# Decoder kernel, last stage: the first LayerNorm half before the feed-forward inside attention batch 3, the second layer's products between the first layer's tiles, and the last LayerNorm in parts of 512, 256 and 256 columns

## The reference

```
def _layernorm(x, axis=-1, eps=1e-05):
    m = mean(x); v = var(x)
    return (x - m) / sqrt(v + eps)

# last cross attention, per batch element (4 of them): query x, key and value ctx_512 (1601 rows, 64 wide)
q, k, v = query @ Wq + bq, key @ Wk + bk, value @ Wv + bv
out = softmax(q @ k.T) @ v
x = layernorm(x + out)

# last feed-forward: hidden width 512, no biases, a scale per output column
h = silu(tlin(x, w1)) * tlin(x, w2)
h = gelu(tlin(h, h1))          # exact gelu
h = gelu(tlin(h, h2))
x = layernorm(x + tlin(h, w3))
```

## Time and profile before

| what | value |
|---|---|
| median of three runs | 706.71 us |
| the profiled execution | 703.72 us |
| its span | 701.9 us |
| PE busy | 620.9 us (88%) |
| DVE, ACT, POOL busy | 527.3, 451.0, 205.6 us |
| batch 3 of the last attention | from about 609.5 to 623.6 us of the span |
| feed-forward and last LayerNorm | from about 623.6 us to the end |

### The profile page before, as it was taken

The page is one execution under the profiler, slowest core; times in us unless marked ns, Lnnn a source line. Parts: engine busy times, 40 slices in busy tenths (PEclk is TensorE's granted clock), DMA queues, the critical chain, the costliest instruction groups (busy, mean ns, idle before and its releaser), DMA issues. The chain is left out here.

```text
span 701.9 us, 13641 instructions
## 1 busy us (share of the span) xinstructions
PE 620.9 (88%) x5206; PEld 341.4 (49%) x5207; DVE 527.3 (75%) x706; ACT 451.0 (64%) x814; POOL 205.6 (29%) x277
## 2 busy tenths in 40 slices
PE   8989899999999999999999796998709999978996
PEld 5645433333334333333433375886205556646883
DVE  5369889999999999999945464999298557868432
ACT  3555578888898888888887432655771056566223
POOL 7224532344455577766740030000000000005000
PEclk9999989999999999999999978999968999999998
DMA  8258575555565554544210287451000010000000
GB/s 204 95 148 267 172 227 173 140 116 138 161 157 121 124 138 98 116 96 97 66 36 1 70 299 312 151 166 59 0 2 0 0 46 1 1 1 1 0 1 30
DMA packets 43293, 70.74 MB, mean 101 GB/s; under 512 B 12492, under 2 KB 31652, under 8 KB 42720
## 3 DMA queue, kind: packets, MB, share of 16 engines
q1 hardware_dynamic: 31696, 38.34, 21.0%
q0 software_dynamic: 10928, 29.32, 13.5%
q10 hardware_dynamic: 608, 2.25, 1.4%
HBM read 44.41 MB, written 24.79 MB: 99 GB/s over the span
## 5 line engine op out<-in xcount | busy, mean ns | idle before, releaser
L962 ACT ACTIVATE prob<-ps 128x512 f32<-128x512 f32 (+2 forms) x480 | 253.1, 582 | 45.9 <-PE ps L738 38.8
L1083 DVE TENSOR_REDUCE pm<-ps 128x2 f32<-128x1024 f32 x192 | 225.8, 1215 | 6.6 <-PE ps L700 4.8
L761 PE MATMUL ps<-prob,vst 128*9 128x256 f32 (+1 forms) x1664 | 129.8, 384 | 10.2 <-ACT o_all L950 10.2
L738 PE MATMUL ps<-qq,kc 50*128 50x256 bf16 (+1 forms) x832 | 134.3, 275 | 0.1
L700 PE MATMUL ps<-kc,qq 48*128 48x512 bf16 x384 | 116.4, 388 | 2.9 <-DVE pm L1083 2.6
L738 PEld LDWEIGHTS ps<-qq,kc 50*128 50x128 bf16 (+1 forms) x832 | 52.1, 96 | 94.0 <-ACT prob L962 69.3
L761 PEld LDWEIGHTS ps<-prob,vst 128*9 128x9 f32 (+1 forms) x1664 | 25.1, 88 | 51.7 <-ACT prob L962 39.1
L1635 POOL DMA_DIRECT2D w_w<-in_w x2 | 1.1, 534 | 148.1 <-PE ps L1672 148.1
L1090 DVE TENSOR_REDUCE nm<-ps 128x4 f32<-128x512 f32 (+1 forms) x32 | 30.6, 958 | 14.9 <-PE ps L688 14.9
L700 PEld LDWEIGHTS ps<-kc,qq 48*128 48x128 bf16 x384 | 32.9, 93 | 13.2 <-DVE pm L1083 9.4
L688 PE MATMUL ps<-masks_b 64*128 64x256 bf16 x256 | 37.6, 269 | 0.0
(11 more groups left out here) (362 smaller groups left out, 1292.3 us busy)
## 6 DMA issues: line engine op xcount, KB each, us to landing
kc<-kc_scr SPq DMA_DIRECT2D x32, 300.2 KB, 5.0
comb_bc<-comb_scr SPq DMA_DIRECT2D x7, 512.0 KB, 4.7
below<-rden_scr POOLq DMA_DIRECT2D x13, 256.0 KB, 6.0
ctx<-ctx_scr POOLq DMA_DIRECT2D x1, 3204.0 KB, 15.0
raw<-in_wexp POOLq DMA_DIRECT2D x8, 384.0 KB, 3.9
exp_scr<-raw_high POOLq DMA_DIRECT2D x8, 384.0 KB, 3.5
exp_scr<-raw_low POOLq DMA_DIRECT2D x8, 384.0 KB, 4.4
kc_scr<-hi SPq DMA_DIRECT2D x6, 400.2 KB, 4.8
```

What stands on the lines that cost most here:

```text
L738: last = pe.matmul(bank[0:p, j * TQ:(j + 1) * TQ], kc[s][rows, j, t * 128:t * 128 + p], qq[s][rows, 0, j, :], start=(j == 0), stop=True, s ...
L761: last = pe.matmul(o_ps[32 * hh:32 * hh + VW, kind * TQ + q0:(kind + 1) * TQ], value[:, hh * VW:(hh + 1) * VW], prob[0:k, (NST * n + t) % ...
L962: act.activation(prob[0:p, g % P_RING, 2 * e:2 * e + 2, q0:TQ], s2[0:p, k % S2_RING, 0:2 * w].rearrange("p (i q) -> p i q", i=2), ACT.Exp, ...
L1083: dve.tensor_reduce(pm[:, m % 2, c, :, jt], banks, AX.X, ALU.max).then_inc(s1_read, 1)
```

## The change

1. `pe_ln5(0)` and `pe_ln5_v(0)`, with the Square on ACT, go from batch 3 into batch 2 (steps 4 and 5); Ln and Exp stay in batch 3, after step 0, and DVE's part goes from step 3 to step 1. Two weight pieces move: piece 5 from batch 3 step 0 to batch 2 step 4 (ACT) and from step 1 to batch 2 step 5 (DVE), piece 6 from step 1 to step 2 and from 2 to 3.
2. DVE does `gated(0)` (gate and high part of tile 0) before batch 3's reciprocal instead of after the residual.
3. up(2) goes before `pe_ln5(1)`, up(3) before `pe_ln5_v(1)`; behind it come tiles 0 and 1 of the first layer, interleaved: 24 matmuls that wait for one `ha_done` after the other. Only then up(4) to up(7). DVE's `dve_ln5(1)` and `split_x(1)` go from before gate 2 to before gate 4. The PSUM banks are dealt anew, and first-layer tile 2 waits for `full_done` 7, which is gate 6.
4. The last layer's half 0 (12 matmuls) goes before second-layer tile 6, its residual behind DVE's tile 5, ln6's centring of it between tiles 6 and 7, its Square on ACT before the last Gelu, its averaging behind tile 7. Half 1 is done in two parts of 256 columns: 24 matmuls of 256 columns in place of 12 of 512, two residuals, and each LayerNorm instruction twice at 256 columns. ACT runs Ln and Exp of half 0 first, with a table load for each, and goes back to the Ln table for the second half: four table loads where there were two. The store is three DMAs instead of two.

The core of the diff (`ln_parts` only learns to take a list of column ranges and views, `spans`):

```diff
-        HIGH_AT = {(1, 0): (0,), (1, 2): (1,), (1, 4): (2,), (2, 0): (3,), (2, 2): (4,), (3, 0): (5,), (3, 1): (6,)}
-        LOW_AT = {(1, 1): (0,), (1, 3): (1,), (1, 5): (2,), (2, 1): (3,), (2, 3): (4,), (3, 1): (5,), (3, 2): (6,)}
+        HIGH_AT = {(1, 0): (0,), (1, 2): (1,), (1, 4): (2,), (2, 0): (3,), (2, 2): (4,), (2, 4): (5,), (3, 2): (6,)}
+        LOW_AT = {(1, 1): (0,), (1, 3): (1,), (1, 5): (2,), (2, 1): (3,), (2, 3): (4,), (2, 5): (5,), (3, 3): (6,)}
-        UP, H1, H2, Y = ((0, 2), (4, 5), (6, 7)), (1, 3), (6, 7), (0, 2)
+        UP = ((0, 2), (4, 5), (1, 3), (0, 2), (1, 3), (6, 7), (0, 2), (1, 3))
+        UP_FREED = (None, None, None, 1, 3, None, 4, 5)
+        H1, H2 = (4, 5, 0, 2), (6, 7)
+        ends = [slice(0, CH), slice(CH, CH + CH // 2), slice(CH + CH // 2, 2 * CH)]
...
-                        if b == NB - 1 and p == 0:
+                        if b == NB - 2 and p == 4:
                             pe.wait_ge(s1_red, 2 * NB)
                             pe_ln5(0)
-                        if b == NB - 1 and p == 2:
+                        if b == NB - 2 and p == PAIRS - 2:
                             pe_ln5_v(0)
...
-                for k in range(1, len(tiles)):
-                    up(k)
-                    if k == 1:
-                        pe_ln5(1)
-                    if k == 2:
-                        pe_ln5_v(1)
...
+                def first_hidden(k):
+                    pe.wait_ge(ha_done, NM * (tiles[k][0] + 1))
+                    if k < 4:
+                        pe.wait_ge(full_done, 7)
+                    else:
+                        pe.wait_ge(g1_done, k - 3)
+                    for i in range(NM):
+                        done = hidden_part("h1w", ha, H1[k % 4], k, i)
+                    done.then_inc(h1_ps, 1)
...
+                def last_layer(n):
+                    end = ends[n]
+                    c = end.start // CH
+                    at = slice(end.start - c * CH, end.stop - c * CH)
+                    for i in range(NM):
+                        pe.wait_ge(hc_done, NM * c + i + 1)
+                        done = passes(Y[n], (high_w["w3"][:, i, :], low_w["w3"][:, i, :]), 0,
+                                      [part[:, i, at] for part in hc[c]], i == 0, i == NM - 1)
+                    done.then_inc(y_ps, 1)
+
+                up(1)
+                up(2)
+                pe_ln5(1)
+                up(3)
+                pe_ln5_v(1)
+                pe.wait_ge(full_done, 2)
+                for i in range(NM):
+                    pe.wait_ge(ha_done, i + 1)
+                    for k in range(2):
+                        done = hidden_part("h1w", ha, H1[k], k, i)
+                        if i == NM - 1:
+                            done.then_inc(h1_ps, 1)
+                for k in range(NM, len(tiles)):
+                    up(k)
+                for k in range(2, len(tiles)):
+                    first_hidden(k)
                 pe.wait_ge(split, split_by["h2w"])
...
+                for k in range(6):
+                    second_hidden(k)
+                last_layer(0)
+                second_hidden(6)
                 pe_ln(0)
+                second_hidden(7)
+                pe_ln2(0)
+                last_layer(1)
+                last_layer(2)
                 pe_ln(1)
-                pe_ln2(0)
+                pe_ln(2)
                 pe_ln2(1)
+                pe_ln2(2)
...
                 act.preload_act_table_set("natural_log")
-                act_ln(0)
-                act_ln(1)
                 act_log(0)
-                act_log(1)
                 act.preload_act_table_set(EXP_LN)
                 act_exp(0)
+                act.preload_act_table_set("natural_log")
+                act_ln(1)
+                act_ln(2)
+                act_log(1)
+                act_log(2)
+                act.preload_act_table_set(EXP_LN)
                 act_exp(1)
+                act_exp(2)
...
                     dve.tensor_copy(osb[:, b % 2, :], o_ps[:, 0:TQ]).then_inc(o_sb, 1)
+                    if b == NB - 1:
+                        gated(0)
                     dve.wait_ge(fin_ps, b + 1)
```

More of the change, by code:

```diff
@@ L112, in ln_parts @@
                 stack, *[f"{tag}_{n}" for n in ("centred", "squared", "var", "lnv", "rstd", "x")])
+            columns = spans or [slice(c * CH, (c + 1) * CH) for c in range(NCH)]
+            if not spans:
+                psum_c, psum_v = ([p[:, c, :] for c in range(p.shape[1])] for p in (psum_c, psum_v))
             def pe(c):
                 nc.tensor.wait_ge(r_ready, c + 1)
-                nc.tensor.matmul(psum_c[:, c, :], mean_out, R[:, c * CH:(c + 1) * CH],
+                nc.tensor.matmul(psum_c[c], mean_out, R[:, columns[c]],
                                  start=True, stop=True).then_inc(centred, 1)
@@ L1625, in _ @@
             def _(sp):
-                for c in range(NCH):
+                for c, end in enumerate(ends):
                     sp.wait_ge(x_ready, c + 1)
-                    sp.dma_start(out[:, c * CH:(c + 1) * CH], X[:, c * CH:(c + 1) * CH]).then_inc(stored, 16)
-                sp.wait_ge(stored, 16 * NCH)
+                    sp.dma_start(out[:, end], X[:, end]).then_inc(stored, 16)
+                sp.wait_ge(stored, 16 * len(ends))
             @block.gpsimd
@@ L1847, in _, with hidden_part @@
-                hidden("h1w", ha, ha_done, H1, g1_done, h1_ps)
-                pe.wait_ge(split, split_by["h2w"])
-                hidden("h2w", hb, hb_done, H2, g2_done, h2_ps)
-                for c in range(NCH):
-                    pe.wait_ge(hc_done, NM * (c + 1))
-                    for i in range(NM):
-                        done = passes(ps[:, Y[c], :], (high_w["w3"][:, i, :], low_w["w3"][:, i, :]), 0,
-                                      [part[:, i, :] for part in hc[c]], i == 0, i == NM - 1)
-                    done.then_inc(y_ps, 1)
+                def hidden_part(name, src, bank, k, i):
+                    c, m = tiles[k]
+                    return passes(ps[:, bank, :], (high_w[name][:, i, :], low_w[name][:, i, :]), m,
+                                  [part[:, i, :] for part in src[c]], i == 0, i == NM - 1)
@@ L2171, in row, with gated @@
                     dve.tensor_copy(shift[:, b % 2, :], fin[:, 0:TQ]).then_inc(row_sb, 1)
+                def gated(k):
+                    c, m = tiles[k]
+                    dve.wait_ge(sg_done, k + 1)
+                    if k >= 4:
+                        dve.wait_ge(ha_done, k - 3)
+                    dve.scalar_tensor_tensor(out=whole[:, k % 4, :], in0=ps[:, UP[k][1], :],
+                                             scalar=col[f"s2_{m}"], in1=sg[:, k % 2, :], op0=ALU.mult,
+                                             op1=ALU.mult).then_inc(full_done, 1)
+                    dve.wait_ge(full_done, k + 1)
+                    dve.tensor_copy(ha[c][0][:, m, :], whole[:, k % 4, :]).then_inc(high_done, 1)
                 phases(0)
```

87 lines of the change are left out of this document (43 added, 44 removed).

## The result

The changed kernel took 697.66 us (median of 11 runs, 694.63 to 700.88) where the kernel before took 704.30 us (11 runs, 700.82 to 708.05): a ratio of 0.9904, 95% interval 0.9875 to 0.9933. So the two traces agree with the sum and the runs do not, and most of what follows is about that difference.

A forecast was written before the change was run, and what follows sets the result against it. PE bounds the dense stretch (busy 55.50 of 55.50 us), followed by a serial 10.30 us tail. The terms, −1.1 to tile 7's end and −3.0 in the tail, sum to −4.1: median 702.6 us, range 700.4 to 706.0.

The forecast's parts named there:

- Handover +1.1: LayerNorm half 0 moved into batch 2 delays batch 3's first Exp by 1.1 us, from 610.24 to 611.3.
- Batch 3 −3.8: Batch 3's Exps of steps 0 and 3 move from 9.26 to 5.44 us apart, saving 3.8 us; up(0) at 620.9.
- Gate 0 +0.65: Gate 0 ahead of batch 3's reciprocal on DVE delays the reciprocal by 0.65 us, to 624.5.
- TensorE's gaps: Up(2) and 24 first-layer matmuls fill PE's waits before the centring and up(4); PE's place in its list gains 5.4 us.
- New wait +0.6: PE waits 0.6 us at first-layer tile 2 for gate 6.
- End of tile 7: Second-layer tile 7 ends at 684.9 instead of 685.96, 1.1 us earlier, despite 3.75 us of last-layer work moved ahead.
- Tail −3.0: From the end of second-layer tile 7 to the last X, 10.4 us instead of 13.4, 3.0 us less.
- B: Rival: DVE and GpSimd pace the middle; interleaved products lose 1.0 us, tile 2 waits 1.2; 704.2 us; chance 0.24.
- C: Rival: LayerNorm matmuls delay batch 3, whose PE-ACT back and forth stays 9.26 us; 707.4 us, slower; chance 0.05.
- D: Rival: tail table loads cost more than their rows; 1.0 us more each takes the whole gain; chance 0.02.
- E: Rival: more gain, no wait at first-layer tile 2 and a tail of 9.9 us; −5.2 us, 701.5 us; chance 0.14.
- the level: The median of the runs lies 3.0 us above the profiled execution of 703.72 us; this difference was carried over unchanged.

The follow-up runs named there:

- no_c1: The changed kernel with its last layer in two halves of 512 again and one tail table load instead of two: 694.82 us, ratio to before 0.9891.
- no_c: The changed kernel with its last layer in two halves of 512 columns again: 696.43 us, ratio to before 0.9895.
- only_a: The kernel before with part 1 alone (LayerNorm half 0 and weight pieces moved into batch 2): 698.09 us, ratio 0.9928.
- one_set: The changed kernel with one tail table load, of a set with both Ln and Exp, instead of four: 694.91 us, ratio to before 0.9870.
- only_b: The kernel before with parts 2 and 3 alone (gate 0 earlier, up tiles and first-layer products reordered): 700.62 us, ratio 0.9968.
- only_c: The kernel before with part 4 alone (divided last layer, four table loads): 706.19 us, ratio 1.0019.
- fill_c: The kernel before with part 4 and eight unused products in TensorE's wait ahead of up(4): 703.61 us, ratio to before 1.0004.
- fill_ab: The kernel before with unused products in TensorE's waits in batch 3 and ahead of up(4): 702.36 us, ratio 0.9974; second sample 702.75 us, 0.9987.
- fill_b: The kernel before with eight unused products in TensorE's wait ahead of up(4): 704.23 us, ratio 1.0000.
- bef4: An unchanged copy of the kernel before, for one more trace: 138.42 us from the residual ahead of the block to the last X.
- bef2: An unchanged copy of the kernel before, for one more trace: 141.43 us from the residual ahead of the block to the last X.

## Why the prediction was right, and where it was wrong

The steps, each with 0.53 us taken off the time in the trace after:

- *Handover +1.1.* Batch 3's first Exp: 611.82 − 0.53 − 610.24 = 1.05. Right.
- *Batch 3 −3.8.* 5.41 us between the Exps, 5.44 forecast. Right; up(0) at 620.8, 620.9 forecast.
- *Gate 0 +0.65.* Reciprocal at 624.3 (624.5), behind tile 0's cast. Right.
- *TensorE's gaps.* The centring at 627.1 (627.3), behind 0.58 us idle instead of 1.0; no wait for the low parts from GpSimd, none at up(4). Right.
- *New wait +0.6.* There, at the place named, but smaller: the row has 0.26 idle, and from start to start it is 0.65 us where a product in a row takes 0.23, so 0.42 lost.
- *End of tile 7.* 684.71 − 0.53 = 684.2, where 684.9 was forecast. Of the 0.7 us the new wait has 0.3 (tile 2 starts 6.03 us behind up(4), forecast 6.3); the rest is spread over several steps.
- *Tail −3.0.* From the end of tile 7 (684.71) to the last X it was 10.75 us, forecast 10.4. The matmuls of 256 columns stood 0.12 us apart (the last twelve in 1.43), not 0.167, which was the spacing of the attention's scores; as the prediction said, that moved nothing, since ScalarE's loads were the later branch: Square at 6.15 us behind tile 7, 6.1 forecast. The 0.3 us were lost behind it.
- *Rivals.* B needed a wait for GpSimd in the interleaved products, C Exps 9 us apart, D time behind a load: none is in the trace. The next instruction starts 0.01 us behind each load, and a load less gained 1.39 us in no_c1, of which 1.28 are the load. E had no new wait and a tail of 9.9: neither came, and the measured 697.66 is below even E's 701.5.
- *The last part's balance.* The steps had it as +3.75 and −3.0, a loss of 0.75 us; no_c measured 0.9.

Sum in the trace −4.43, forecast −4.1. Of the 0.7 us gained ahead of tile 7's end the tail took 0.35 back; that the rest is so small is in part luck. The direction, to which the prediction gave 0.61, was right. What failed is what the sum was laid upon.

The first step that failed is the level: "The median of the runs is 3.0 us above it; I carry the difference over unchanged." The 706.71 was a median of three; four later samples of before (80 runs) have medians of 703.6 to 704.7. With 704.3 the same −4.1 gives 700.2. That is 2.4 us of the 4.9, and this failure is shown.

The second is a term that isn't in the sum. The prediction priced the waits in batch 3 by the time that they lasted in one trace and put what may follow them at nothing: it has no term for the granted clock, of which it read one row, 1.00 from 636.10 us on. Two of five traces of before have 1.2 GHz for 6.8 us behind them, at 3.04 us each; the nine traces with these waits (before and the edits that keep them) have it three times, the nine where the waits are gone or filled never. If that is the share in the runs, it makes 2/5 of 3.04, 1.2 us, in the mean of before, an estimate, which the change would give back beside what its instructions save: 4.43 + 1.2 = 5.6 us, where 23 runs gave 5.9. The same sum fits the others: only_a 2.77 + 1.2 = 4.0 (measured 5.1, from 3.4), no_c 6.6 (0.9907; 0.9895), one_set 8.2 (0.9883; 0.9870), no_c1 8.0 (0.9887; 0.9891), only_b, which keeps the waits, 2.5 alone (0.9964; 0.9968). Even without the share of two in five the pattern stands: the nine samples whose kernels lack the waits or have them filled gained 0.5 to 2.3 us more in the runs than in the stretch; the four that keep them between −0.4 and 0.7 (only_c and fill_c counted at their stretch without the fall). The profiled trace of before was one without the fall, so the durations read from it were right and its total was still no mean.

How firm that is: that a fall costs 3.04 us in before is read from traces, twice. That the waits bring it is argued, not shown: it rests on three of nine against none of nine, which chance alone would give about once in ten times, on the pattern of the surpluses, and on fill_ab's gain, of which one interval excludes 1 and one does not quite. The share of two in five is from five traces.

A further number bears on it: for every run there is its mean granted clock. In 128 runs of kernels with batch 3's waits (before, only_b, only_c, fill_b, fill_c) it is 0.9660 on average, in 71 of kernels without them or with fillers 0.9676. The difference, 0.0016 ± 0.0013, is about what fewer falls would do (6.8 us at half the clock in two of five executions are 0.0019). But the changed kernel alone has 0.9660 in 23 runs, against 0.9663 in 80 of before, ± 0.0015: that shows no fewer falls. So for the changed kernel the 1.2 us are not confirmed, and a gain of its untouched part is not excluded; the traces cannot tell, since the stretch starts at 560.1 us on average with the waits and at 559.5 without, each with a scatter of 1.5 us.

Why one execution falls and the next, with the same waits, does not, is open. The last 1.3 us between forecast and result are within what medians of the changed kernel differ by (697.66, 698.32, 699.28).

## What to carry to other kernels

Read more than one trace of the kernel before pricing a wait on TensorE, since what follows a wait can be slower in some executions, and a trace in which it wasn't shows only the wait itself. Compare traces between two instructions that both have, not by their spans, and take the level from many runs. Count the table loads of a change that divides a LayerNorm: here the division moved work to where TensorE is full, added two loads and cost 0.9 us, while one set for both functions gained 2.6 with the division and 1.4 without it.

## What the runs showed of the hardware

- In two executions of one kernel with waits equal to 0.01 us (bef4 and bef2), TensorE's granted clock was 1.00 in one and 0.50 for 6.8 us in the other, which was 3.0 us longer.
- Useless products in its waits made a kernel 1.8 us faster (0.2 to 3.5) and, in a second sample, 0.9 us (−0.4 to 2.3).
- Matmuls of 256 columns started 0.12 us apart where those of 512 took 0.233, each with other weights: half the columns, half the time. The products of the attention's scores, 256 columns too, took 0.67 us for four, 0.167 each; the runs do not show why.
- A table load took 1.28 us in the rows read here, and where the next instruction waited for nothing else it started 0.01 us behind (686.91, 688.91 and 690.86 above); one load less on the chain shortened the stretch by 1.39 us.
